# A two-layer transformer kernel on one core: all value products of a step of four slots in one group

## What is computed

```python
scores = jnp.einsum('bhld,bhmd->bhlm', q, k) * scale + gb[None]
probs = jax.nn.softmax(jnp.where(causal[None, None], scores, -jnp.inf), axis=-1)
elastic = jax.nn.relu(probs + tau[None, :, None, None] / row[None, None, :, None])
out = jnp.einsum('bhlm,bhmd->bhld', elastic, v)          # the value products
x = x + out.reshape(B, L, D) @ Wo.T + L0_ffn(xn)         # layer 0
x = x + L1_attn(xn) + L1_ffn(xn)                         # layer 1
```

## Time and profile before

| | before |
|---|---|
| median of three runs | 2256.84 us |
| the profiled execution | 2258.64 us |
| its span, first to last instruction | 2256.8 us |
| PE busy | 2052.5 us, 91% |
| DVE, ACT, POOL busy | 1584.0, 1449.5, 1149.8 us |
| mean granted clock of TensorE | 0.982 of full speed |

### The profile page before, as it was taken

One profiled execution on the slowest core, in us unless ns is written; L12 is line 12 of the kernel. 1 busy time (PEld: TensorE's weight loads), 2 busy tenths in 40 slices (PEclk: granted clock), 3 DMA queues, 4 the chain that ended last, 5 costly groups with the idle time before them and its releaser, 6 DMA issues.

```text
span 2256.8 us, 52525 instructions
## 1 busy us (share of the span) xinstructions
PE 2052.5 (91%) x18761; PEld 1347.9 (60%) x18761; DVE 1584.0 (70%) x5288; ACT 1449.5 (64%) x3925; POOL 1149.8 (51%) x1800
## 2 busy tenths in 40 slices
PE   3888999999899998989999998998999999899988
PEld 2455665756566575655656566575656657566555
DVE  6557767677776867767686776767777686775646
ACT  2767575675757667575666757667575665757542
POOL 5675463744637465463745636364463645535220
PEclk8779999999999999999999999999999999999999
DMA  4000000000000000000000000000000000000000
GB/s 122 6 6 2 1 16 2 15 2 14 2 2 15 2 16 1 2 16 1 16 1 16 2 1 15 2 16 2 4 13 2 15 1 11 2 2 11 2 10 6
DMA packets 33542, 22.03 MB, mean 10 GB/s; under 512 B 2443, under 2 KB 32771, under 8 KB 33283
## 3 DMA queue, kind: packets, MB, share of 16 engines
q1 hardware_dynamic: 33283, 18.68, 2.9%
HBM read 14.48 MB, written 4.19 MB: 8 GB/s over the span
## 4 chain that ended last, share of the span: by engine, by line
PE 51%; DVE 19%; ACT 14%; POOL 8%; issue 8%; DVEq 0%; ACTq 0%; POOLq 0%
PE ps L1109 8%; PE ps L1249 8%; PE ps L1180 8%; PE ps L1190 6%; ACT ring L921 5%; DVE ring L540 4%; PE ps L1123 4%; PE ps L1099 3%; POOL ring L814 3%; ACT pb L930 3%; PE ps L1168 2%; PE ps L1234 2%; PE ps L1156 2%; DVE lin L577 2%; PE ps L1087 2%
## 5 line engine op out<-in xcount | busy, mean ns | idle before, releaser
L814 POOL TENSOR_SCALAR ring<-ring,row_rcp,tau_row 128x128 f32<-128x128 f32 (+3 forms) x1024 | 629.9, 623 | 825.0 <-DVE row_rcp L547 824.9
L921 ACT ACTIVATE ring<-ring,neg_max 128x128 f32<-128x128 f32 (+3 forms) x1024 | 572.9, 561 | 514.3 <-DVE neg_max L540 510.8
L1109 PE MATMUL ps<-identf,ring 128*128 128x128 f32 x2560 | 380.0, 287 | 18.4 <-ACT qkT L912 11.3
L930 ACT ACTIVATE pb<-ps 128x512 f32<-128x512 f32 x640 | 350.1, 587 | 26.2 <-PE ps L1109 18.2
L1109 PEld LDWEIGHTS ps<-identf,ring 128*128 128x128 f32 x2560 | 279.5, 143 | 96.6 <-issue 55.0
L540 DVE CUSTOM_DVE_ANT_1 ring<-ps,bias_t 128x384 f32<-128x384 f32 (+1 forms) x496 | 287.0, 614 | 67.7 <-PE ps L1099 63.8
L1249 PEld LDWEIGHTS ps<-ed_t,h 128*128 128x128 f32 (+1 forms) x1920 | 250.7, 191 | 74.7 <-issue 73.1
L1180 PE MATMUL ps<-xn1T,eg_t 128*128 128x512 f32 (+1 forms) x480 | 257.6, 618 | 23.8 <-DVE h L594 23.7
L1249 PE MATMUL ps<-ed_t,h 128*128 128x128 f32 (+1 forms) x1920 | 272.3, 278 | 0.0
L1190 PE MATMUL ps<-xn1T,eu_t 128*128 128x512 f32 (+1 forms) x480 | 257.4, 618 | 12.7 <-ACT vx L893 12.4
L944 ACT ACTIVATE tanh_t<-ps 128x512 f32<-128x512 f32 (+2 forms) x304 | 172.7, 568 | 117.1 <-PE ps L1180 112.5
(11 more groups left out here) (162 smaller groups left out, 3206.6 us busy)
## 6 DMA issues: line engine op xcount, KB each, us to landing
x_t<-x SPq DMA_DIRECT2D x16, 256.0 KB, 2.8
x<-x SPq DMA_DIRECT2D x16, 256.0 KB, 2.8
out<-x SPq DMA_DIRECT2D x16, 256.0 KB, 2.3
bias_t<-bias SPq DMA_DIRECT2D x1, 1536.0 KB, 7.6
eg_t<-eg SPq DMA_DIRECT2D x1, 860.0 KB
eu_t<-eu SPq DMA_DIRECT2D x1, 860.0 KB
ed_t<-ed SPq DMA_DIRECT2D x2, 320.0 KB
ring<-inv_row SPq DMA_DIRECT2D x1, 256.0 KB, 2.7
```

What stands on the lines that cost most here:

```text
L814: pool.tensor_scalar(e, e, row_rcp[:, m % 2, r:r + 1], tau_row[:, i, HG * g + r:HG * g + r + 1], ALU.mult, ALU.add).then_inc(p_ok.sem, 1)
L921: act.activation(e, e, ACT.Exp, bias=neg_max[:, n % 2, r:r + 1], scale=-1.0, accum_out=row_sum[:, n % 2, r:r + 1]).then_inc(exp_ok.sem, 1)
L930: act.activation(pb[:, c % NPB, :], bank(turn_bank(q)), ACT.Relu).then_inc(t_taken[q % 2].sem, 1)
L1109: last = pe.transpose(o[:, r * P:(r + 1) * P], ring_of(i, r)[:, k * P:(k + 1) * P], idf)
```

## The change

`blocks_before` returns nothing in three of a step's four slots, and in the first slot of a step all blocks of the step before. It is called by PE's program (value products) and by ACT's (`store_o`, which copies the sum of a group of heads after its last block).

```diff
     def blocks_before(self, f, s):
 
-        near, far = (self.blocks(*divmod(SLOTS * f + s - back, SLOTS)) for back in (2, 4))
-        return [blk for blk in far if STEPS[blk[1]][1] == 0] + [blk for blk in near if STEPS[blk[1]][1]]
+        if s % HG:
+            return []
+        return [blk for back in (4, 2) for blk in self.blocks(*divmod(SLOTS * f + s - back, SLOTS))]
```

## The result

The changed kernel takes **2264.22 us** (median of 5 runs, 2263.71 to 2270.09) against 2256.84 before (5 runs beside it): ratio **1.0037**, 95% interval 1.0020 to 1.0053. It is slower by 0.37%, inside the range of 2247 to 2270, 5.7 us above the number forecast, and just past the 0.3% that would have been no change. Run again, the same kernel gave 1.0035 (1.0022 to 1.0048). The profiled execution took 2263.71 (span 2261.9), that of before 2258.64 (2256.8).

A forecast was written before the change was run, and what follows sets the result against it. PE bounds only stretches, taking turns with DVE, ACT and POOL. Terms of -0.03 + 0.03 - 0.10 + 0.21 + 0.00 = +0.11 us a frame, +1.7 over 15, gave 2260.3, less 1.8 for the runs' median: 2258.5 us, range 2247 to 2270.

The forecast's parts named there:

- what a group costs: PE's value products: a block costs 0.22 us, being a group 0.13 to 0.14; groups of 24 and 32 take 0.79 and 1.01.
- The two signs by which the mechanism was to be judged: PE's wait for DVE at pair 23 grows, and DVE's idle time before `lin` in pair 19 falls from 0.38.
- pairs 23, 31, 16: Places where PE waits: 0.57 taken out in 23 and 31, 0.57 added in 16; each was to change the time by 0.
- pair 19: Products taken out; PE reaches `lin` 0.57 earlier, but DVE was idle only 0.38 before it: -0.38 us.
- Pair 17: Products taken out, -0.57 for PE, but DVE works without a gap to the end of its `lin`: -0.53 us taken.
- Pair 11: Path of turning, ACT's store, ACT's copy of v, PE: turning earlier brings ACT's store 0.09 forward, -0.09 us.
- Pairs 0 and 1: Start of the next frame, beside POOL's full stretch: PE's +0.57 and -0.57 were to cost 0 each.
- pair 12: 0: +0.44 on PE makes ACT run 0.35 late, but DVE has some 0.19 to spare beyond that: 0.
- Pair 20: +0.44, in full: In PE's own stretch, 16 records added to a group of 16 cost their whole 0.44 us.
- PE decides: Rival: PE's saved work counts on the path, 16.8 us in full; 2240 us in full, 2248 for half; chance 0.2.
- ACT decides: Rival: ACT's delays in first pairs exceed DVE's and POOL's spare time, 0.75 a frame, 11 us: 2270 us; chance 0.22.
- The free boundary: Rival: group boundaries cost PE nothing, so open insertions cost 0.13 more each, 0.9 a frame, 14 us: 2272; chance 0.04.

The follow-up runs named there:

- the filler: Five kernels with 8 or 16 records of value products put into PE's wait ahead of pair 20's scores; ratios to the kernel before 0.9976, 0.9968, 0.9935, 0.9974, 0.9963.
- the eight-step kernel: Only steps 1, 2, 3, 5, 6, 9, 10, 11 of sixteen merged, nothing filled, against the kernel before: 2250.03 us, ratio 0.9970.
- again: The changed kernel run once more, nothing altered, against the kernel before: 2265.02 us, ratio 1.0035.
- all but step 7: The changed kernel with step 7's blocks left in two groups as before, against the kernel before: 2248.90 us, ratio 0.9940.
- one filling: The changed kernel with step 7's first two blocks multiplied once more in pair 19's wait, against the kernel before: 2255.64 us, ratio 0.9976.
- six steps: Only steps 2, 3, 6, 9, 10, 14 of sixteen merged, against the kernel before: 2253.08 us, ratio 0.9967.
- the late blocks alone: The kernel before, with only step 7's first two blocks moved behind pair 19's `lin`, into PE's wait: 2252.42 us, ratio 0.9974.
- one block: Changed kernel, value products multiplied once more in two PE waits: one block (8 records) in pair 19, two blocks in pair 9; against before: 2250.49 us, ratio 0.9963.
- step 7 alone: The kernel before with only step 7 of sixteen merged, its first two blocks moved from pair 19 to pair 20: 2273.54 us, ratio 1.0056.

## Why the prediction was right, and where not

**The size and the direction.** 2264.2 lies in the range and on the side of the forecast's sign (+1.7 forecast, +7.4 measured), but past the bound of "no change", at 0.37% against 0.3%. The statement that the 17 us saved on PE would not come back as time held, and the pair-by-pair account held for most pairs within 0.05 us. For a good part the total was met by errors that go against each other, and that was luck.

**Right: what a group costs.** The group of 24 now takes 0.79 (615.09 to 615.88) and that of 32 takes 1.01, as read from the layer-1 product. A boundary is not free; pairs 18, 26, 28 and 4 pay 0.43 to 0.48 for 16 records more, not 0.57.

```profile
615.09 0.86 PE L1124 MATMUL ps<-pb,vx 128*32 128x128 f32 x24
615.88 1.09 PE L1110 MATMUL ps<-identf,ring 128*128 128x128 f32 x8
```

**Right: taken out into waits.** The two signs by which the mechanism was to be judged both came (PE's timeline of the changed kernel, pairs 23, 31, 16):

```profile
645.45 1.12 PE L1181 MATMUL ps<-xn1T,eg_t 128*128 128x512 f32 x2 [1.55 <-DVE h L595]
...
680.76 0.83 PE L1143 MATMUL ps<-wo_t,v_future 128*16 128x128 f32 x6 [0.79 <-DVE neg_max L541]
...
606.62 0.65 PE L1124 MATMUL ps<-pb,vx 128*32 128x128 f32 x16
607.20 1.09 PE L1110 MATMUL ps<-identf,ring 128*128 128x128 f32 x8
```

Pair 23's wait grew from 1.11 to 1.55 and pair 31's from 0.22 to 0.79, at no gain; the wait of 0.36 for ACT's stack copy in pair 16 is gone. In pair 19 DVE's idle time before its `lin` has shrunk from 0.38 to 0.15, too little for the view to list (622.78 + 1.12 = 623.90 to 624.04):

```profile
622.78 1.12 DVE L670 SCALAR_TENSOR_TENSOR x<-ps,comb,x 128x128 f32<-128x128 f32 x4
624.04 1.29 DVE L578 TENSOR_TENSOR lin<-ps,tri_t 128x512 f32<-128x512 f32 x2
```

**Small misses.** Pair 19 gave 0.23, not 0.38: I let `lin` use all of DVE's idle time. The expert's sum ahead of it starts 1.61 behind the pair's first score in both traces (1030.70 and 622.78), so it is no earlier; the `lin` starts 3.10 behind it before and 2.87 now, and 0.15 of idle time stays between the two. By the record PE's last product for it now ends at 623.67, before the expert's sum does; what holds the `lin` for the 0.15 is not shown. Pair 17 takes 4.36 in every frame now; before, it takes 4.93 in seven of thirteen frames and 5.11 in six, so the median's -0.58 stands beside a mean of -0.66. Pair 11 gave 0.21, not 0.09. Pairs 0 and 1 do feel the +0.57 and -0.57 on PE, where I had them covered, but the sum is 0 as forecast. The largest lies in "pair 12: 0": the added 0.44 does reach the next pair, and a wait there pays it, the 0.43 for DVE's L594 at 1140.03 in the trace of before (first line). Now the same product, of the same shape, follows without one:

```profile
1140.03 1.13 PE L1180 MATMUL ps<-xn1T,eg_t 128*128 128x512 f32 x2 [0.43 <-DVE h L594]
...
733.32 0.39 PE L1088 MATMUL ps<-ident,kx 128*128 128x128 f16 x4
733.74 1.12 PE L1181 MATMUL ps<-xn1T,eg_t 128*128 128x512 f32 x2
```

In pair 14 another 0.19 comes free, of a wait of 0.44 for DVE. So an undisturbed frame is 134.44 against a median of 134.70, -0.26 and not +0.11. The error is one of covering: I looked for what a delay costs on ACT and DVE, and not for how far those had come earlier through pair 11.

**The step that failed: "Pair 20: +0.44, in full".** It is +0.44 in six frames and +2.01 in nine. I took PE's clock as given, and the window of that stretch as one in which PE is busy; I did not look at the waits inside it as places where the clock might fall. The mechanism named for pair 19 (PE runs ahead, DVE follows by part) was right. What is left over is a longer wait, and I wrote that a longer wait costs nothing. In pairs 23 and 31 that is so (the clock fell in neither, at 1.55 and 0.79), in pair 19 it is not. Nine times 1.57 is 14.1 us, more than any term of my sum. It was none of the rivals, and it is larger than the forecast's edge; that the range held owes as much to the gain that I missed (0.26 + 0.11 a frame, 5.6 us in fifteen) and to the opening (4.5 us). The falls alone on top of my number would have given 2258.5 + 14.1 = 2272.6, outside the range; that it held is luck.

**The rivals.** PE decides: refuted as it stood (a full gain of 0.75% never showed), though the undisturbed frames lean a little to its side. ACT decides: refuted, since pairs 12 to 14 and 0 and 1 sum to 0 or less. The free boundary: refuted by 0.79 and 1.01 above, so the rule of the Trainium skill, "TensorE: Matmul & The Clock Gate", Part 2, step 5, does not hold between these groups.

## What to carry to other kernels

Work that stands in front of a wait is not always dead weight: before taking it out, list the waits that grow by it, and read the granted clock by window, pair or tile, in each of the repeated frames and not in one. When a change slows some frames and not others by the same amount, compare a long one with a short one inside the same trace; the records name the place. A trace without falls does not show that a place is safe, as its frames may all have come at harmless moments. Where a clock fall is the cause, a few true matmuls moved into the wait are worth more than the same work saved (here 16 records: 0.26% faster moved, 0.46% slower left out).

## What the runs showed of the hardware that was not expected

A PE that is 90% busy, whose single waits are about 1 us, can still lose its clock: 0.51 from 626.53 to 629.93, after a wait of 1.12 and shorter ones. It came in 41 of 60 frames with 1.12 unfilled, in 7 of 60 with 0.77, in none of 75 with the filler. It is not a matter of the wait alone: the eight-step kernel has pairs 19 and 20 as before and fell in 5 frames of 15, by when they came; and the changed kernel's wait of 1.55 in pair 23 has no fall behind it in any frame. Why pair 23 is spared was not tried. The Trainium skill, "TensorE: Matmul & The Clock Gate", section "A second HAM failure mode: psum-queue depth-cycling", tells of a kernel in which frequent short idle times between groups of matmuls were enough for the clock to go down and up again; this trace agrees that short idle times can do it, here single waits of 0.77 and 1.12. In the opening of every kernel whose windows were read (before, changed, again, all but step 7, one filling) the granted clock is low over some 100 us as well (0.62 to 0.84 in stretches of 40 us).

**Open.** That a frame's place against the beat decides was read from thirteen traces and tested by no run that shifts the frames alone. The falls in pair 9 (with one filling, six steps and eight steps) bunch in the same way, but unfilled frames without a fall lie among them; there the cause is less clear. The profiled execution of before has no fall in pair 20, but its runs spread over 2254.0 to 2263.5, and putting true work into pair 19's wait gained 0.1% more than the pairs account for. The runs' mean granted clock goes with their time (0.983 and 0.984 in the three runs at 2254.0, 0.977 in the one at 2263.3), so lost clock is in that spread; whether it is lost in pair 20 or in the opening can't be seen without their traces. Pair 17 is 0.2 longer in eight of fifteen frames of before, in seven of the late blocks alone and in eight of one block, and pair 9 is 0.51 longer in one frame of before and four of step 7 alone, without a fall; both unexplained.
